# A decoder layer on one core: both stages in one program block, and the last stage's step written in a new order

## What is computed

```
x = x + attn(layernorm(x))      # 16 heads of 128: silu(x W_qkv), decayed causal scores (no softmax),
                                # out = norm_w * o * rsqrt(mean(o*o)); (sigmoid(x W_gate) * out) W_out
x = x + xattn(layernorm(x))     # scores against 64 context rows, softmax, readout; rows masked per batch
x = x + ffn(layernorm(x))       # 512 -> 1408 -> 512; inputs, hidden values and weights rounded to 8-bit floats
                                # with a scale per row; t = silu(g) * u; y = q(t) W_down
```

## Time and profile before

| | us |
|---|---|
| median of 3 runs | 2817.42 |
| the profiled execution's own time | 2816.95 |
| its span, first to last instruction | 2815.2 |
| attention's last output passes start | 1986.1 |
| first pass of the output projection starts | 1997.9 |
| last pass of the output projection starts | 2713.7 |
| one step of the tail in its steady part (2499.91 to 2522.87, the last pass of a quarter to the same pass a step later) | 22.96 |

### The profile page before, as it was taken

How to read it: one execution, slowest core, us unless ns; L and a number is a source line. 1 busy time by engine, 2 the same in 40 slices (tenths; PEclk the granted TensorE clock), 3 DMA queues, 4 the chain that set the end, 5 groups by cost and what they waited for, 6 DMA issues and landing times. The chain is left out here.

```text
span 2815.2 us, 40631 instructions
## 1 busy us (share of the span) xinstructions
PE 2679.2 (95%) x14711; PEld 2202.4 (78%) x14711; DVE 2171.2 (77%) x3814; ACT 1126.9 (40%) x1880; POOL 840.8 (30%) x823
## 2 busy tenths in 40 slices
PE   6999999999999999999999999999699999999985
PEld 6888888888888888888888888888566666666652
DVE  7888877877787787788888678676458888888875
ACT  4433233433433343343444224222235555555553
POOL 3111111311221121121212102101036666666665
PEclk9999999999999999999999999999799999999997
DMA  6562333333243243224334223322633433444310
GB/s 228 201 214 92 124 118 124 130 114 128 98 151 121 102 129 143 97 101 177 111 118 171 93 92 143 140 90 105 227 117 109 118 117 112 118 123 120 113 42 19
DMA packets 119014, 350.99 MB, mean 125 GB/s; under 512 B 15776, under 2 KB 18720, under 8 KB 110112
## 3 DMA queue, kind: packets, MB, share of 16 engines
q1 hardware_dynamic: 116480, 339.74, 35.2%
q0 software_dynamic: 2336, 8.65, 0.9%
HBM read 251.75 MB, written 96.61 MB: 124 GB/s over the span
## 5 line engine op out<-in xcount | busy, mean ns | idle before, releaser
L556 PE MATMUL bank<-attention_xT,attention_w_hi 128*128 128x512 f32 x3072 | 956.8, 392 | 3.0 <-DVE attention_xT L757 2.6
L556 PEld LDWEIGHTS bank<-attention_xT,attention_w_hi 128*128 128x128 f32 x3072 | 568.1, 188 | 116.2 <-issue 3.6
L556 PE MATMUL bank<-attention_xT,attention_w_lo 128*128 128x512 f32 x1536 | 600.9, 391 | 0.0
L415 POOL TENSOR_TENSOR attention_sq_sum<-attention_sq_sum,attention_sq 128x512 f32<-128x512 f32 x128 | 206.2, 1611 | 1251.9 <-ACT attention_sq L538 1251.9
L565 PE MATMUL bank<-attention_w_hi,attention_xT 128*128 128x256 f32 x2048 | 381.5, 287 | 3.7 <-DVE attention_sig_v L714 3.7
L1219 PE MATMUL bank<-finish_w_out_hi,finish_og 128*128 128x512 f32 x1024 | 356.8, 411 | 21.9 <-DMA finish_og<-gated_heads 16.3
L556 PEld LDWEIGHTS bank<-attention_xT,attention_w_lo 128*128 128x128 f32 x1536 | 288.5, 188 | 62.7
L565 PEld LDWEIGHTS bank<-attention_w_hi,attention_xT 128*128 128x128 f32 x2048 | 319.3, 192 | 3.9 <-DVE attention_sig_v L714 3.9
L565 PE MATMUL bank<-attention_w_lo,attention_xT 128*128 128x256 f32 x1024 | 290.4, 284 | 0.0
L847 DVE TENSOR_TENSOR attention_sf<-bank,attention_dcy 128x512 f32<-128x512 f32 (+1 forms) x256 | 147.7, 619 | 171.3 <-PE bank L649 171.2
L1219 PEld LDWEIGHTS bank<-finish_w_out_hi,finish_og 128*128 128x128 f32 x1024 | 195.7, 191 | 67.9 <-DMA finish_og<-gated_heads 16.8
(11 more groups left out here) (195 smaller groups left out, 5054.9 us busy)
## 6 DMA issues: line engine op xcount, KB each, us to landing
attention_xT<-normed_turned SPq DMA_DIRECT2D x62, 2048.0 KB, 8.6
gated_heads<-attention_og_out SPq DMA_DIRECT2D x64, 1024.0 KB, 7.6
finish_og<-gated_heads SPq DMA_DIRECT2D x128, 512.0 KB, 3.8
normed_turned<-shared SPq DMA_DIRECT2D x24, 512.0 KB, 6.8
shared<-in_w_head SPq DMA_DIRECT2D x16, 512.0 KB, 7.2
finish_x<-in_x SPq DMA_DIRECT2D x32, 256.0 KB, 4.3
out<-finish_x SPq DMA_DIRECT2D x32, 256.0 KB, 4.3
attention_x_in<-in_x SPq DMA_DIRECT2D x5, 1024.0 KB, 9.8
```

Source lines behind the costliest of these rows:

```text
L415: g.tensor_tensor(sq_sum[:, col_b], sq_sum[:, col_b], sq[:, :], ALU.add).then_inc(s_acc, 1)
L556: mm = pe.matmul(dst[:, :], part[a][w][:, k, col:col + P], xT[i][:, b, k, :], start=(k == 0 and s == 0), stop=(k == KD - 1 and s == 2))
```

## The change

Both stages now write their instructions into one `Block`, so that no meeting of the engines stands between them. What made this possible in memory is a map by hand (`memory_map`): each tile of either stage has a fixed address, and waits (`attention_over`) guard the addresses that the second stage takes over.

Within the last pair of heads:

- The output weight is split: ScalarE makes the high parts 0 to 3 in slots 114, 116, 118 and 120, parts 4 to 6 in slot 126, part 7 in slot 127. GpSimd, and not VectorE, makes the low parts, in place in `shared`: parts 0 to 3 a slot later each, 4 to 6 at the start of slot 126, part 7 after the last sum of squares.
- SyncE loads the first four quarters of heads and four tiles of x in slot 126; those before waited for the second block.
- The last `sum_squares`, the roots and the feed-forward weights' loads follow the first projections: `up` in step -3, `gate` in step -2, `down` in step -1.

In the tail's step:

- Silu is one function of ScalarE (`ACT.Silu`). `sigmoid` followed by GpSimd's multiplication `silu` is gone: GpSimd has three products a tile fewer.
- The order is new on all engines, and steps are `range(-3, T + 3)`: TensorE projects tile n + 3 and runs `down` for tile n - 3, so six tiles lie between the two.
- `turn_t` and `t_turned` are cut in two; GpSimd's `rstd` for two tiles at a time is cut into `rstd2` and `rstd3`, `norm_stats` into `norm2_stats` and `norm3_stats`, `x_round` into two.

The core of the diff; the rest of it is the indentation of code that left its block, and names of tiles:

```diff
+        with nc.Block() as block:
+            @block.sync
+            def _(sp):
+                first.sync(sp)
+                second.sync(sp)
...
+            if n == LAST - 1:
+                sp.wait_ge(s_g, n)
+                for Q in range(early.RING - 1):
+                    load_heads(sp, Q)
+                sp.wait_ge(s_o, n)
+                for m in range(4):
+                    load_tile(sp, m)
...
+            if n - 1 in SPLIT:
+                w_out_lo(SPLIT[n - 1])
+            if n == LAST - 1:
+                for q in range(4, PARTS - 1):
+                    w_out_lo(q)
...
+    def attention_over(eng):
+
+        eng.wait_ge(early.s_ogl, early.HEADS)
+        eng.wait_ge(early.s_sq, early.HEADS)
+        eng.wait_ge(early.s_acc, early.HEADS)
...
-                def sigmoid(m, i):
-                    k, (a, w) = m * NF + i, FS[i]
-                    act.wait_ge(s_g, k + 1)
-                    if k >= 2:
-                        act.wait_ge(s_gs, k - 1)
-                    nc.scalar.activation(sg[k % 2][:, 0:w], g_[k % 2][:, 0:w], ACT.Sigmoid).then_inc(s_sig, 1)
...
+        def silu(m, i):
+            k, (a, w) = m * NF + i, FS[i]
+            act.wait_ge(s_g, k + 1)
+            after(act, s_t, k - 1)
+            nc.scalar.activation(sg[k % 2][:, 0:w], g_[k % 2][:, 0:w], ACT.Silu).then_inc(s_gs, 1)
...
+        for n in STEPS:
+            if tile(n + 1):
+                add_readout(n + 1)
+                norm3_stats(n + 1)
...
+            if tile(n - 3):
+                y_scaled(n - 3)
+            if tile(n + 1):
+                x_scale(n + 1)
+            if tile(n - 1):
+                t_scale(n - 1)
+            if tile(n):
+                scaled_gate_up(n, 0)
+            if tile(n + 3):
+                add_attention(n + 3)
...
+            if tile(n):
+                scaled_gate_up(n, 2)
+            if tile(n - 1):
+                t_round_out(n - 1)
```

2523 lines of the change are left out of this document (1298 added, 1225 removed).

## The result

The changed kernel takes 2724.14 us (median of four, 2721.92 to 2728.08), the kernel before 2817.52 (now the median of four as well). The ratio is 0.967, 95% interval 0.9654 to 0.9687: 93 us less, where 79 were forecast. The profiled execution was the longest of the four, 2728.08 us, with a span of 2726.3; its sums are made against that.

A forecast was written before the change was run, and what follows sets the result against it. TensorE was taken to bound the kernel. Attention's end 1989.4, filling 93.2 and steps 566.8 reach 2649.4; the last projection at 2646.8, drain 86.3, 3 for small waits and 1.8 from span to time give 2738, range 2722 to 2774.

The forecast's parts named there:

- attention's end: End of attention's last output pass: 3 us later, through GpSimd's three subtractions in slot 126 beside VectorE, at 1989.4.
- filling, to `turn_h(5)`: Six filling steps after attention, each TensorE's 21.8 without parts lacking a tile: 93.2 us together, plus 3 for small waits.
- 26 steady steps: Steps 3 to 28 of the tail, set by TensorE's own work at 21.8 us each: 566.8, to 2649.4.
- the last projection's end: TensorE's last projection ends 2.6 us before the steady steps do, at 2646.8, where it was 2714.0.
- drain: Rounds after the last projection: 83.3 us plus 3 for passes at half clock, 86.3 together, where it was 101.2.
- So 1.2 us are to spare: Steady step: the chain from `turn_h` through Silu and `exp` takes 8.4, ending at 25.1; `turn_p` wants it at 26.3.
- the step does not get shorter: Rival, chance 0.12: in the steady step another wait takes the place, the step stays at 22.9, +29 us, 2767.
- the loop over three engines: Rival, chance 0.05, slower than before: ScalarE, GpSimd and VectorE's 18 us loop plus waits exceeds the step; 2826 at 25.2.
- The rival from the Trainium skill: Rival, chance 0.02: ScalarE's table switches cost 1.38 more each, `turn_p` waits 1.4 to 1.6 a step, +39 us, 2777.
- The rival that the transfers hold it up: Rival, chance 0.07: while filling, `gate_up(0)` or the heads wait for transfers as before, tile 6 gains nothing, +39 us, 2777.
- the forecast's 40, 29 and 15, less 5 of allowances: Gains making up 79 us: 40 from change of stage and filling, 29 from steady steps, 15 from drain, less 5.
- what it has to do takes 22.95 - 3.9 = 19.0: VectorE's own work in a steady step, its 3.9 us of waits taken off: 19.0, leaving 2.7 to spare below 21.8.

The follow-up runs named there:

- the second profile: The changed kernel run again unchanged, as the measure for other runs on the same chip: 2724.69 us (2722.73 to 2726.85), ratio 0.9666.

## Why the prediction was right, and where its sum was off

The time lies in the range (2722 to 2774), at its lower end, 14 below the 2738 forecast, and it moved the way forecast, by 93 in place of 79. The sum, term by term, in the profiled execution:

| term | forecast | measured | off by |
|---|---|---|---|
| attention's end | 1989.4 | 1992.4 | +3.0 |
| filling, to `turn_h(5)` | 109.1 (93.2 + 15.9), + 3 allowed | 113.8 | +4.7 - 3 |
| 26 steady steps | 566.8 | 564.0 | -2.8 |
| the last projection's end | 2646.8 | 2651.8 | +4.9 |
| drain | 86.3 | 74.5 | -11.8 |

With the allowance this gives 2738 - 9.9 = 2728.1; the median of the four is 3.9 lower than the execution that was profiled. The errors have both signs, so part of the closeness is luck: the first stages came 4.7 later than forecast, the steps and the drain 14.6 shorter.

**The steady step** was right in what sets it and in its size. The order of the earlier trace rows gave 0.81 for `turn_t` and 0.46 for `turn_p`. Silu alone took away 0.80, and the order took away both, to 21.69, at the lower of the bounds, 21.7 and 22.0. That 21.8 and not 21.7 was taken cost 2.8. "So 1.2 us are to spare" ahead of `turn_p` had the right sign and the wrong size: the prediction's chain has a table load ahead of Silu as well as ahead of `exp`, and in the new order only the second lies between `turn_h` and `turn_p`. The chain takes 6.8 and not 8.4 (2497.35, the start of `h_turned`, to 2504.15, the end of `exp`), and `turn_p` starts at 2507.02, 2.9 later. TensorE waits for nothing there, even with the three products back on GpSimd. With that the rival "the step does not get shorter" falls, and the loop over three engines too: it has room for 4.8 us of GpSimd more. The rival from the Trainium skill (ScalarE: Activation LUTs, What ACT_TABLE_LOAD costs) is not decided by that: with one switch and 2.9 to spare, its 1.38 more a switch would not have made `turn_p` wait either. It falls by ScalarE's own order of time, in which nothing stands ahead of the load or behind it:

```profile
2501.79 0.61 ACT L1278 ACTIVATE finish_silu<-finish_g 128x512 f32<-128x512 f32 x1
2502.42 1.28 ACT L1308 ACT_TABLE_LOAD   x1
2503.72 0.35 ACT L1308 ACTIVATE finish_pr<-finish_sc,finish_softmax 128x64 f32<-128x64 f32 x1
```

**Attention's end** was right in its cause and the cause's size: +3 was forecast, and it is 3.4. The last slot is 2.6 longer, as three subtractions beside VectorE make it, and 0.8 more comes from its `scores` at half clock behind a wait of 2.4. The other 2.6 were there before the 127th `scores` (a start 3.4 later, less 0.8 on the way), and 2.2 of them were not there in the second profile.

**The change of stage** was right in its causes: the early loads, the single block and the order of the transfers were each undone, for 6.3, 5.8 and 11 us. The fill was 1.7 longer than forecast with its allowance, mostly the wait of 3.15 for `add_attention(0)` and the passes at half clock behind it; 1.2 had been counted, with the roots but not the landing of the mask ahead of them. The rival that the transfers hold it up fell for this order of loads; for the old one it would have been right in kind, but at 11 and not 39. The prediction spoke of 40 us for this part. The measure that goes with its other two, 25 steps and the drain, gives 30.5: 88.9 in all, less 31.7 (25 x 1.27) and 26.7 for the drain. So the forecast's 40, 29 and 15, less 5 of allowances, stand beside 30.5, 31.7 and 26.7: too much for the first, too little for the last.

**The drain** is the term that was mis-sized, 74.5 for 86.3. One step of the prediction has most of it: "what it has to do takes 22.95 - 3.9 = 19.0. The change adds next to nothing to it". VectorE's 19.0 held over 2 us in which it waited inside its own instructions for GpSimd (it is 16.5 now). In the steady step this cost nothing, as TensorE sets it; the first rounds of the drain go at VectorE's pace. The `t_round_out` there were forecast 18, 17, 12.3 and 10.3 apart after a first part of 11.6; they came 15.5, 16.7, 11.6 and 9.3 apart after 9.3, 6.8 less together. The first part and the first round have 4.8 of this, and VectorE has no idle time in that round. In the later three it waits again, 1.4 for `down`, 1.3 for GpSimd and 3.0 for `t_scaled`, and 2.0 are left in which its own work and GpSimd's shorter queue are not told apart. With the three products back on GpSimd the same five are 9.6, 18.4, 17.3, 15.2 and 11.6. The contention is not all gone either: `t_round_sum` takes 1.85 and 2.32 in two of the rounds after, 1.62 alone. The remaining 5.0 lie behind the last `t_round_out`, 12.2 where 17.1 stood (14.1 and the 3 for passes at half clock). The 3 were not needed: one `down` took 4.83 and its round was still shorter than forecast. `down(31)` ran at full clock, 2.55 for 3.89 before, which is 1.3 more. Rows 7 had shown the contention at the output weight, and the prediction used it there; it was not looked for in the durations of the tail, where 2.57 for 128x1408 stands one instruction behind 1.61 for the same shape.

What stays open: how much of the change of stage the hand-made map brings by itself (blocks, loads and order were undone one by one, the map never), why the start varies by up to 3.4 and the way to the 127th `scores` by as much, and what the masks ahead of the roots cost.

## What to carry to other kernels

Where two instructions of one engine have the same shape and unlike durations, the longer one holds a wait for somebody: take it out before the duration goes into a sum, above all for a stage that goes at this engine's pace. Two parts of a change that remove the same wait are worth less together than apart, so undo each in the new kernel as well as doing it alone in the old. At a change of stage, loads asked for ahead, no meeting of the engines and the order of the transfers were each worth 6 to 11 us with the others in place; what comes behind a wait of TensorE pays once more in clock, and where it must wait for a short time, passes that nothing uses can pay. A meeting also waits for the slowest engine's last work: look there before its cost is put down to the meeting. And before a rival is called refuted by a wait that did not come, count the slack there from the new trace.

## What the runs showed of the hardware

- VectorE and GpSimd hold each other up for whole instructions: 128x1408 bf16 from two tiles in SBUF took 1.61 alone, 1.90 and 2.57 beside products, and a 128x384 product 0.99 alone and 2.38. The tail's operations of 128x512 that read one input from a bank kept their time (0.73 to 0.75 in both kernels, one of them, at 2515.56 in the kernel before, beside a product).
- It works the other way round and for small instructions too: a GpSimd operation of 128x1 that takes 0.19 alone took 1.48 beside `t_round_sum` (at 2504.91 and 2504.73 in the kernel after).
- Not only operations with two inputs lose by it: a plain `CAST` of 128x512 took 1.87 in place of 0.43 beside a subtraction on GpSimd.
- With a meeting of all engines between two blocks TensorE stood for 8.0 us; its first pass came 2.7 after the last engine, GpSimd, had ended its work.
- A wait of 3.25 on TensorE was followed by a granted clock of 0.62 over 5 us and by a `down` of 4.19 in place of 2.55; with 20 passes in the place of the wait the clock was 1.00.
